# Carried scan states in 32-partition groups by pairs of chunks, and their products on row tiles of TensorE

## The reference, cut to what matters

```python
dA = jnp.exp(dt[:, :, None, :] * A[None, :, :, None])
dB = dt[:, :, None, :] * Bt
def step(h, inp):
    dA_t, dB_t, x_t, C_t = inp
    h = dA_t[:, :, None, :] * h + dB_t[:, :, None, :] * x_t[..., None]
    y_t = jnp.einsum('bhds,bhs->bhd', h, C_t)
    return (h, y_t)
```

## Time and profile before

| | |
|---|---|
| median of 3 runs | 1727.96 us (1727.75 to 1729.5) |
| profiled execution | 1728.12 us, its span 1726.3 us |
| TensorE busy | 1643.1 us (95%), weight loads 925.4 us |
| VectorE busy | 1169.5 us (68%) |
| ScalarE busy | 890.0 us (52%) |
| GpSimd busy | 404.1 us (23%) |
| chain that ended last | TensorE 82%, VectorE 11%, ScalarE 3%, issue 3% |

### The profile page before, as it was taken

The page is one execution under the profiler, slowest core; times in us unless marked ns, Lnnn a source line. Parts: engine busy times, 40 slices in busy tenths (PEclk is TensorE's granted clock), DMA queues, the critical chain, the costliest instruction groups (busy, mean ns, idle before and its releaser), DMA issues.

```text
span 1726.3 us, 24435 instructions
## 1 busy us (share of the span) xinstructions
PE 1643.1 (95%) x8693; PEld 925.4 (54%) x8693; DVE 1169.5 (68%) x2480; ACT 890.0 (52%) x1091; POOL 404.1 (23%) x415
## 2 busy tenths in 40 slices
PE   4688999999999999999999999999999999999988
PEld 3254654555545655456545565456554565545643
DVE  6779776567756676547775578566775577653765
ACT  4647453475355653555544754457525564446532
POOL 0304311044021431233220430204302142113310
PEclk9789999999999999999999999999999999999999
DMA  6303410144102431224211441024310243112301
GB/s 206 99 0 105 147 28 14 74 134 141 41 25 83 127 115 41 75 67 154 75 21 74 129 147 28 17 80 139 128 41 34 86 131 99 40 50 78 112 13 49
DMA packets 140719, 140.17 MB, mean 81 GB/s; under 512 B 68900, under 2 KB 118116, under 8 KB 140591
## 3 DMA queue, kind: packets, MB, share of 16 engines
q1 hardware_dynamic: 126542, 103.18, 19.4%
q0 software_dynamic: 12288, 34.68, 6.1%
q10 hardware_dynamic: 1760, 0.64, 0.2%
HBM read 78.46 MB, written 60.01 MB: 80 GB/s over the span
## 4 chain that ended last, share of the span: by engine, by line
PE 82%; DVE 11%; issue 3%; ACT 3%; DMA 1%; POOL 0%; DVEq 0%; SPq 0%; POOLq 0%; ACTq 0%
PE bank L1626 77%; PE bank L1794 2%; PE bank L1925 2%; DVE bn L915 1%; DVE gate L1138 1%; PE bank L1844 1%; DVE scan_tmp L1498 1%; ACT L713 1%; DVE wmax L885 1%; DMA x_even<-in_x 1%; ACT work L567 1%; DVE work L1578 0%; ACT buf_a L564 0%; PE bank L1696 0%; DVE scan_tmp L1500 0%
## 5 line engine op out<-in xcount | busy, mean ns | idle before, releaser
L1626 PE MATMUL bank<-buf_a,win_hi 128*128 128x512 f16 x1536 | 460.7, 382 | 8.1 <-DVE buf_a L987 8.1
L1626 PE MATMUL bank<-buf_a,win_lo 128*128 128x512 f16 x768 | 292.7, 381 | 0.0
L1626 PE MATMUL bank<-buf_b,w_hi 128*128 128x512 f16 x960 | 288.1, 382 | 2.4 <-DVE buf_b L987 2.4
L1626 PEld LDWEIGHTS bank<-buf_a,win_hi 128*128 128x128 f16 x1536 | 148.5, 99 | 174.9 <-DVE buf_a L987 10.9
L465 POOL DMA_INDIRECT d_scan<-rows,rank x128 | 126.6, 989 | 347.3 <-ACT rows L648 304.6
L1626 PE MATMUL bank<-buf_b,w_lo 128*128 128x512 f16 x480 | 182.9, 381 | 0.0
L481 POOL DMA_INDIRECT rows<-d_y,rank x128 | 131.1, 1025 | 205.4 <-DMA d_y<-buf_b 164.7
L1626 PE MATMUL bank<-buf_a,w_hi 128*128 128x512 f16 x576 | 171.3, 379 | 1.5 <-DVE x_odd L1230 1.4
L1626 PEld LDWEIGHTS bank<-buf_b,w_hi 128*128 128x128 f16 x960 | 94.0, 99 | 112.6 <-DVE buf_b L987 3.0
L1626 PEld LDWEIGHTS bank<-buf_a,win_lo 128*128 128x128 f16 x768 | 75.6, 98 | 91.9 <-issue 2.2
L1626 PE MATMUL bank<-gate,w_out 128*128 128x512 f32 x256 | 120.3, 603 | 1.1 <-DVE gate L1343 1.1
(11 more groups left out here) (254 smaller groups left out, 3073.1 us busy)
## 6 DMA issues: line engine op xcount, KB each, us to landing
rows<-d_scan SPq DMA_DIRECT2D x16, 1024.0 KB, 6.3
d_y<-buf_b SPq DMA_DIRECT2D x64, 256.0 KB, 2.7
work<-in_x SPq DMA_DIRECT2D x24, 512.0 KB, 4.5
d_gram<-rows SPq DMA_DIRECT2D x32, 260.0 KB, 2.4
x_even<-in_x SPq DMA_DIRECT2D x16, 512.0 KB, 6.3
x_odd<-in_x SPq DMA_DIRECT2D x16, 512.0 KB, 6.0
out_x<-x_even SPq DMA_DIRECT2D x16, 512.0 KB, 2.7
out_x<-x_odd SPq DMA_DIRECT2D x16, 512.0 KB, 2.6
```

The costliest lines, as they stand in the source:

```text
L1626: return eng.matmul(out, lhsT, rhs, start=start, stop=stop, skip_group_check=True, **kw)
```

## The change

The group that reaches over the whole chunk now depends on the pair of chunks: group 4j for chunks 2j and 2j+1, so that its 8 states lie in partitions 32j to 32j+7 of the transposed factors. The carried state of a pair is kept in those partitions, and the carried products take 32 rows instead of 128, at partitions 0, 32, 64 or 96. The far columns of `pfac` are weighted into a tile of their own, `p_far`, and then set to zero in `pfac`. All seven state products of a head go to one bank, between the two halves of the `pT` by `qT` products. In `scan_y` the chunk products come first, four at a time, and the carried ones after them. Three banks instead of two serve the units q17 to q23; steps of the input projection are placed elsewhere (28 as before), and the start of the output projection has another order.

```diff
-FAR_GROUP = (0, 0)
+PAIRS = NT // 2
+far_group = lambda c: 4 * (c // 2)
...
-        gam = sb("gam", [S, HEADS, NT])
-        a_col = sb("a_col", [S, HEADS])
+        gam = sb("gam", [P, HEADS, NT])
+        a_col = sb("a_col", [P, HEADS])
+        p_far = sb("p_far", [P, NT, S])
...
-        yt_bank = ((3, 5), (4, 6), (3, 3), (4, 4))
-        dh_bank = lambda c: (3, 4, 0, 0)[c // 2]
-        m_bank = 5
+        yt_bank = ((5, 4), (3, 6), (3, 3), (4, 4))
+        dh_bank = 6
+        m_bank = 3
+        y_bank = (5, 3, 4, 6)
         factor_bank = (3, 5)
-        in_bank = (3, 4, 6, 1, 2, 1, 2, 1, 2, 1, 4, 5, 6, 3, 2, 1, 4) + (2, 1) * 3 + (2,)
-        out_bank = (0, 2, 1, 5, 6, 0, 3, 4)
+        in_bank = (3, 4, 6, 1, 2, 1, 2, 1, 2, 1, 4, 5, 6, 3, 2, 1, 4, 2, 0, 1, 2, 0, 1, 2)
+        out_bank = (0, 1, 2, 5, 6, 0, 3, 4)
...
@@ ScalarE, image @@
                 scan_y(0, 3)
                 scan_factors(1)
-                filler(2)
+                filler(3)
                 for j in range(4):
                     scan_y(1, j)
                 filler(1)
                 y_high(m, 0)
                 y_high(m, 1)
                 filler(1)
                 y_high(m, 2)
-                filler(1)
                 y_high(m, 3)
...
@@ VectorE, scan_factors @@
+                far = bass.AP(pfac.tensor, pfac.offset, [list(pfac.ap[0]), [2 * P + 4 * S, PAIRS], [P, 2], [1, S]])
                 wait(eng, "fac_exp", m, 3 * h + 1)
+                TT(p_far[:, :, :].rearrange("p (j b) s -> p j b s", b=2), far, wgt.rearrange("p (j b) s -> p j b s", b=2),
+                   ALU.mult).then_inc(s["fac_pq"], 1)
+                wait(eng, "fac_pq", m, 5 * h + 1)
+                eng.memset(far, 0.0).then_inc(s["fac_pq"], 1)
+                wait(eng, "fac_pq", m, 5 * h + 2)
                 TT(p4, p4, wgt.unsqueeze(2).broadcast_to([P, NT, G, S]), ALU.mult).then_inc(s["fac_pq"], 1)
...
@@ VectorE, scan_states @@
-                    wait(eng, "dh_mm", m, 4 * h + c // 2 + 1)
+                    if c == 0:
+                        wait(eng, "dh_mm", m, h + 1)
...
-                        STT(hst[hp, c, :], hst[hp, c - 1, :], gam[:, h, c:c + 1], inc, ALU.mult, ALU.add).then_inc(s["h_st"], 1)
+                        STT(hst[hp(c), c, :], hst[hp(c - 1), c - 1, :], gam[hp(c - 1), h, c:c + 1], inc, ALU.mult, ALU.add).then_inc(s["h_st"], 1)
...
@@ TensorE, scan_sums @@
-                    mm(b7[0:S, 320:328], const("ones")[:, 0:S], r[:, :, DH], True, True).then_inc(s["fac_mm"], 1)
+                    mm(b7[:, 320:328], const("ones"), r[:, :, DH], True, True).then_inc(s["fac_mm"], 1)
...
+                def state_products(h):
+                    wait(eng, f"scanx{h}", m, 16)
+                    for c in range(NT - 1):
+                        ins = mm(ps[dh_bank][32 * (c % 4):32 * (c % 4) + S, (c // 4) * DH:(c // 4 + 1) * DH],
+                                 p_far[:, c, :], rows4[:, h, c, 0:DH], True, True)
+                    ins.then_inc(s["dh_mm"], 1)
                 def scan_inner(h):
-                    state_products(h, range(0, 4))
                     for half in range(2):
                         wait(eng, "fac_ptq", m, 4 * h + (3 if half == 0 else 4))
+                        if half:
+                            state_products(h)
                         for c in range(4 * half, 4 * half + 4):
                             ins = mm(ps[m_bank + half][:, (c % 4) * P:(c % 4 + 1) * P], pT[:, c * P:(c + 1) * P],
                                      qT[:, c * P:(c + 1) * P], True, True)
                         ins.then_inc(s["mm_m"], 1)
-                    state_products(h, range(4, NT - 1))
...
@@ TensorE, scan_y @@
+                    def carried(c):
+                        rows_of_pair = slice(32 * (c // 2), 32 * (c // 2) + 32)
+                        return mm(out(c), qT[rows_of_pair, c * P:(c + 1) * P], hst[rows_of_pair, c - 1, :], False, True)
+                    for half in range(2):
+                        wait(eng, "m_ev", m, 2 * h + half + 1)
+                        if half:
+                            wait(eng, "h_st", m, 7 * h + 7)
+                        for c in range(4 * half, 4 * half + 4):
+                            mm(out(c), mmat[:, c * P:(c + 1) * P], r[:, c, 0:DH], c % 2 == 0, c == 0)
+                        if half and between:
+                            between()
+                        if half == 0:
+                            wait(eng, "h_st", m, 7 * h + 3)
+                        for c in ((1, 2, 3), (4, 6, 5, 7))[half]:
+                            ins = carried(c)
+                            if c % 2 == 1:
+                                ins.then_inc(s["y_mm"], 1)
...
@@ TensorE, image @@
                 scan_y(0)
+                piece(3)
                 factor_rows(1, 0)
                 piece(2)
                 factor_rows(1, 1)
                 scan_inner(1)
-                piece(2)
+                piece(5)
                 scan_y(1, bound_across)
...
-                piece(4)
+                piece(2)
                 y_chunk(0, 0)
...
                 y_chunk(1, 0)
-                piece(4)
+                piece(2)
                 y_chunk(0, 1)
                 y_chunk(1, 1)
-                piece(4)
+                piece(2)
                 wait(eng, "in_evac", m, 23)
...
                 wait(eng, "y_lo", m, 1)
                 out_part(0, 0)
+                out_part(1, 0)
+                out_part(3, 0)
                 wait(eng, "in_evac", m, 24)
-                out_part(1, 0)
                 out_part(2, 0)
-                wait(eng, "y_gate", m, 3)
                 wait(eng, "y_lo", m, 2)
-                out_part(0, 1)
-                out_part(1, 1)
-                out_part(2, 1)
-                out_part(3, 0)
-                out_part(3, 1)
-                y_chunk(2, 0)
-                y_chunk(3, 0)
+                for u in range(4):
+                    out_part(u, 1)
                 wait(eng, "y_lo", m, 4)
                 out_part(4, 0)
                 out_part(4, 1)
+                y_chunk(2, 0)
+                y_chunk(3, 0)
                 if first:
                     gn_sum(m + 1, 0)
                 wait(eng, "y_res", m, 5)
```

More of the change, by code:

```diff
@@ L43, in constants @@
     blocks = [(s, size) for size in (128, 64, 32, 16) for s in range(0, P, size)]
-    left, right = np.zeros((P, HEADS, G)), np.zeros((P, HEADS, G))
-    keep = np.ones((P, HEADS))
-    for h in range(HEADS):
-        groups = [g for g in range(G) if g != FAR_GROUP[h]]
+    left, right = np.zeros((P, PAIRS, G)), np.zeros((P, PAIRS, G))
+    for j in range(PAIRS):
+        far = far_group(2 * j)
+        groups = [g for g in range(G) if g != far]
         for g, (s, size) in zip(groups, blocks):
-            left[s:s + size // 2, h, g] = 1
-            right[s + size // 2:s + size, h, g] = 1
-        left[:, h, FAR_GROUP[h]] = right[:, h, FAR_GROUP[h]] = 1
-        keep[FAR_GROUP[h] * S:(FAR_GROUP[h] + 1) * S, h] = 0
+            left[s:s + size // 2, j, g] = 1
+            right[s + size // 2:s + size, j, g] = 1
+        left[:, j, far] = right[:, j, far] = 1
     parts["left"], parts["right"] = left, right
     parts["off_left"], parts["off_right"] = BIG * (1 - left), BIG * (1 - right)
-    parts["keep"] = keep
     parts["within8"] = (v[:, None] % T8) <= np.arange(T8)[None, :]
@@ L1507, in scan_factors @@
                 wait(eng, "fac_mm", m, h + 1)
-                wait(eng, "dh_mm", m, 4 * h)
+                wait(eng, "dh_mm", m, h)
                 wait(eng, "fac_tp", m, 4 * h)
@@ L1550, in scan_states, with hp @@
             def scan_states(m, h):
-                far = FAR_GROUP[h] * S
-                hp = slice(far, far + S)
+                def hp(c):
+                    pair = (c + 1) // 2
+                    return slice(32 * pair, 32 * pair + S)
                 def whole_chunks(half):
@@ L1752, in in_step @@
                             wait(eng, "tok_ev", m, 3 if q < 12 else 4)
+                        elif q == 18:
+                            wait(eng, "sp_z", m, 1)
                         elif q > 4:
@@ L1837, in factor_rows @@
                     if h and a == 0:
-                        wait(eng, "y_ev", m, 2)
+                        wait(eng, "y_ev", m, 3)
                     if h and a == 1:
@@ L1841, in factor_rows @@
                     for half in range(2):
-                        wait(eng, "fac_pq", m, 3 * h + 1 + (1 + half if a else 0))
+                        wait(eng, "fac_pq", m, 5 * h + 3 + (1 + half if a else 0))
                         for c in range(4 * half, 4 * half + 4):
@@ L1883, in scan_y @@
                     r = rows4[:, h]
[L1884 to L1898 removed]
+                    out = lambda c: ps[y_bank[c // 2]][:, (c % 2) * DH:(c % 2 + 1) * DH]
+                    def carried(c):
[8 more added lines that the diff above has]
+                        if half and between:
+                            between()
+                        if half == 0:
```

(3 more changed lines are left out.)

64 lines of the change are left out of this document (17 added, 47 removed).

## The result

The kernel before took 1728.45 us in the runs beside this comparison (14 runs), the changed one 1731.96 (1730.77 to 1732.71, 14 runs). The ratio is 1.0019, with an interval of 1.0012 to 1.0026. The profiled execution has a span of 1730.4 us, 4.1 more than before. Lines L1626 and L1925 of before are L1636 and L1934 of after.

The account below looks back on a forecast made before the run. TensorE, busy 1643 of 1726 us, was taken as the bound. Terms of +1.41 per image, 8 x 1.41 - 10.7 = +0.6, plus +1.2 for the first image, gave +1.8: 1729.8 us, own range 1725 to 1735, overall 1717 to 1739.

Parts of the forecast that it names:

- Carried products: Carried products on TensorE: four row-tile batches of 1.36 us replace 14 products, 5.25 against 6.05, 0.80 gained per image.
- Rival C: Row tiles do not overlap, a batch takes 1.68 or 2.10 us: slower, 1747, chance 0.07.
- Far columns: Before `pfac` is weighted, VectorE gets two small operations: +0.46 us per image for head 0, covered for head 1.
- scan_inner: `pT` by `qT` products come first and wait for ScalarE's `qT` copy: +0.14 us head 0, +0.23 head 1.
- Wait for the chunk matrices: TensorE's wait before head 1's products goes: -1.25 us per image, 10.7 over all images.
- Low parts of y: Behind the scan, fewer steps are left as cover, so TensorE waits 0.53 us for VectorE's first low part.
- Order before the float32 parts: Unit 4's parts now precede the transposes, leaving 1.56 us idle before `out_part(0,2)` where 0.26 was: +1.30 per image.
- Transfers of head 1: Gathers of head 1 land about when `y_chunk(2,0)` comes: nothing, up to 0.7 in the range.
- Rival B: Transfers of head 1 become the bound, or a longer stall brings the clock down: slower, 1738, chance 0.18.
- First image: `gated(4)` stands behind the next image's statistics, so the end moves with the one-row matmul (+2.6): +1.2 us.
- Rival A: Weight loads overlap and the 1.56 us idle before `out_part(0,2)` is not there: faster, 1718, chance 0.26.

Follow-up runs that it names:

- e2: The changed kernel with the carried products on all 128 rows again, same order and steps: 1742.52 us, ratio 1.0084 to the kernel before.
- e5: The changed kernel with three steps of the input projection moved to cover three small waits (four in place of five before scan_y(1)): 1724.96 us, ratio 0.9979.
- e6: The kernel before with only y_chunk(2,0) and y_chunk(3,0) moved behind the two parts of output unit 4: 1740.32 us, ratio 1.0068.
- e1: The changed kernel with the transposes y_chunk(2,0) and y_chunk(3,0) put back ahead of the two parts of output unit 4: 1726.47 us, ratio 0.9992.
- e4: The changed kernel with the steps of the input projection placed where they were before the change: 1753.28 us, ratio 1.0145.
- e8: The changed kernel with all eight chunk products first, then the seven carried products of a head in one batch on four row tiles: 1748.53 us, ratio 1.0116.
- e9: e8 with both exp of head 1 ahead of the copies of y of head 0 on ScalarE: 1720.62 us, ratio 0.9954.
- e7: The changed kernel with e1, e5, three x loads issued earlier, and the one-row matmul ahead of the first transposes: 1715.56 us, ratio 0.9929.
- e10: e7 with head 0's carried products in one batch of seven and both exp of head 1 ahead of the copies of y: 1701.27 us, ratio 0.9846.
- e11: e7 with the next image's statistics done later in the first image, behind gated(4) to gated(7) on VectorE: 1718.09 us, ratio 0.9939.

## Why the prediction came out as it did

The forecast was 1729.8, and 1731.96 was measured: the mechanism was the one described, and two terms were mis-sized, in opposite directions. That they lie on opposite sides is luck: the measured batch alone would have made the forecast 1726.5, and the first image alone 1732.0.

- *Carried products.* Foreseen: a batch of 1.36 and 0.80 gained per image. Measured: 1.26, the lower bound, since the weight loads of two tiles overlap; that is 4 x 1.26 - 0.2 = 4.84 against 6.05, 1.2 gained. e2 gives 1.2 to 1.3 per image. Rival C is out.
- *Far columns.* Foreseen +0.46 with a bare load. Measured: a wait of 0.47, and 0.53 until the next step starts (785.84 to 787.24, less the 0.87 of the transposes). The two operations behind it sum to 0.48 (784.55 to 785.03), as VectorE's timeline shows:

```profile
784.55 0.25 DVE L1523 TENSOR_TENSOR p_far<-x_even,rows 128x64 f32<-128x64 f32 x1
784.89 0.11 DVE L1526 MEMSET x_even<- 128x64 f32 x1
785.03 1.23 DVE L1528 TENSOR_TENSOR x_even<-x_even,rows 128x1024 f32<-128x1024 f32 x1
```

- *scan_inner.* Foreseen +0.14 and 0.50 of waiting with the bare load; measured 3.47 (788.54 + 0.87 to 792.88) against 3.27, +0.20; in head 1 it was +0.30 (3.47 against 3.17), and 0.23 was foreseen. The batch of seven state products took 0.98 from start to start.
- *Wait for the chunk matrices.* Foreseen gone, and it is. e5 shows how much was to spare at head 1: one step fewer there brings back 1.7 us in all.
- *Low parts of y.* Foreseen 0.53 (its own figures, 4.74 - 4.26, give 0.48), measured 0.62 in the even images (826.17 + 0.22 to 827.00) and 0.89 in the odd ones.
- *Order before the float32 parts.* Foreseen 1.56 idle, a bare load of 0.107 included; measured 1.45 to the first start in every steady image, 1.56 by the same count, so this term came out exactly. The page sums it to 9.8 us. e6 shows it alone (+11.7) and e1 takes it out (-5.5).
- *Transfers of head 1.* Foreseen nothing, up to 0.7. One image waited for a gather. Rival B did not happen in the changed kernel; e1 shows that it stands right behind.
- *First image.* This is the term that was mis-sized most. It was put at +1.2 over a steady one. The float32 parts of the second image start 3.79 later, of which 0.30 was there before the scan began, so the first image cost 3.5. Up to its own float32 parts that is 2.13 - 0.30 = 1.8, where 2.6 - 1.28 = 1.3 was foreseen. The mechanism was right: `gated(4)` stands behind the statistics on VectorE, and the float32 parts move with the one-row matmul, which is 2.13 late itself (201.93 against 199.80). The clock at 166 us stands in that: in a steady image the one-row matmul is only 1.0 late (822.12 - 817.34, less the 785.84 - 782.09 with which the scan began). The rest comes behind, in two pieces. The stall was not priced as one, 3.14 us of standing still after which the clock stayed at its lower level twice as long (5.27 - 4.37 = 0.9 for six records). And 0.9 is lost at 274.24 us before L1706, which waits for VectorE's product that ends at 274.13, and VectorE had waited for a transfer, 1.1 us longer than before (1.60 at 268.42):

```profile
272.55 0.37 DVE L1186 TENSOR_TENSOR rows<-rows,cst 128x200 f32<-128x200 f32 x1 [2.70 <-DMA rows<-d_norm]
```

SyncE issued that transfer 2.26 us behind the write that it reads, 1.24 before. The wait is 2.4 to 3.1 in every kernel here that holds the change and 1.4 in e6, so it belongs to the change; why the write lands later no run here shows. The text named a long stall and the clock as a risk, under rival B, and looked for it in the steady images alone. There it was right for this kernel: 1.56 left the clock at 1.00. It fell in steady images of e4 and e8, whose longest waits there are 1.8 and 2.7, and once in e9 (1033 to 1035 us), whose longest is 1.45 as here, so the length of one wait alone does not decide it. All later images together cost 0.3; the terms had given 7 x 0.08 = 0.6. The batches gained 7 x 0.4 more than that, and the small terms above (low parts, `scan_inner`, far columns: 0.4 per image together, and one late gather) took it back.

Rival A had half of its mechanism (the loads overlap) and not the other (the idle time before the float32 parts is there); e1, which takes that idle time away, ends below the kernel before by 2 us.

## What to carry to other kernels

A change that makes the bounding engine's work shorter by 10 us can end slower, because each of its waits was covered by the work or the order that the change moved: list the waits that the new order uncovers, one by one, and put a step of independent work ahead of each, as e5 and e7 did. Where operations of another engine stand between a producer and the copy that frees a bank (exp among the copies of y), move what is ready ahead first, and only then make the producer's batch larger, as e9 and e10 did. Together these steps end 31 us below the changed kernel. Price the first and the last image apart from the steady ones, the clock behind each long stall with them, and before moving a stall look at what its instructions feed.

## What the runs showed of the hardware

- On row tiles of 32 partitions, float32 products of 256 columns cost by the busiest tile alone: three, four and seven products on two, two and four tiles took 1.06, 1.06 and 1.07 us from start to next start (e8 for the seven; the busiest tile has two in each), against 1.29 for three and 1.72 for four over all rows (e2).
- The loads of two tiles lie in 0.19 us together, and a batch pays 0.2 once for entering and leaving, not per tile.
- The clock fell behind some stalls and not behind others, and their length alone does not tell which. The sum of statistics waited 2.42 us in e7 and the clock was 1.00 from 215 to 223 us; it waited 3.14 in the changed kernel, and 0.50 followed for over 4 us, as it did behind the 9.8 of e11. But in the kernel before it fell to 0.50 for 3.4 us behind two waits of 0.68 and 1.26, and e7 had a second wait of 1.26 too. Behind the same wait of over 5 us at 157 to 163 us it stayed down twice as long in the changed kernel as before.
- ScalarE's table load of 1.28 us (808.45 in e8) begins only when the exp's turn has come, so an exp between two copies costs 1.28 + 1.06 there, though ScalarE had been idle for 7.99 us. In e9, where no copy of y stands ahead of the exp, the load ran at 788.48, and the exp, which had to wait for its operand until 793.75, then had no load in front of it.
